# Linear stage of a two-layer transformer: the output projection in three bf16 passes on a split gated activation

## The reference

```python
q = jax.nn.softmax(q, axis=-1)
k = jax.nn.softmax(k, axis=1)
ctx = jnp.einsum('bnhd,bnhl->bhdl', k, v)
y = jnp.einsum('bnhd,bhdl->bnhl', q, ctx).reshape(B, T, D)
emb_out = jax.nn.silu(emb) @ emb_W + emb_b
scale, shift = jnp.split(emb_out, 2, axis=-1)
h = layer_norm(y, sn_g, sn_b) * (1.0 + scale) + shift
h = jax.nn.silu(h) @ out_W + out_b
return x + gate_msa * h
```

## Time and profile before

| | us |
|---|---|
| median of three runs | 1329.25 |
| lowest and highest of them | 1326.26, 1334.49 |
| the profiled execution | 1331.78 |
| its span, from first to last instruction | 1330.0 |
| PE busy in the span | 1172.4 (88%) |
| DVE busy | 945.9 (71%) |
| ACT busy | 784.2 (59%) |
| POOL busy | 846.9 (64%) |
| mean granted TensorE clock | 0.968 of full speed |

### The profile page before, as it was taken

How to read it: one execution, slowest core, us unless ns; L and a number is a source line. 1 busy time by engine, 2 the same in 40 slices (tenths; PEclk the granted TensorE clock), 3 DMA queues, 4 the chain that set the end, 5 groups by cost and what they waited for, 6 DMA issues and landing times. The chain is left out here.

```text
span 1330.0 us, 37647 instructions
## 1 busy us (share of the span) xinstructions
PE 1172.4 (88%) x12222; PEld 857.5 (64%) x12222; DVE 945.9 (71%) x2275; ACT 784.2 (59%) x2143; POOL 846.9 (64%) x1026
## 2 busy tenths in 40 slices
PE   3578898989989884699999999996899999999996
PEld 2356777777777773366666666673566666666664
DVE  3857787878878753764645565624899999999984
ACT  1466676777777762345545454632576767777664
POOL 2556677777777754636666666641467676767677
PEclk9789999999999997699999999997999999999999
DMA  5554233232322322100110101010011111111112
GB/s 160 146 125 105 50 58 62 53 60 56 58 61 54 64 54 71 52 17 16 33 32 16 32 16 32 17 33 0 12 32 43 39 51 39 35 55 35 39 55 73
DMA packets 142576, 67.86 MB, mean 51 GB/s; under 512 B 80432, under 2 KB 141232, under 8 KB 142512
## 3 DMA queue, kind: packets, MB, share of 16 engines
q1 hardware_dynamic: 109904, 40.92, 13.8%
q10 hardware_dynamic: 32608, 26.12, 6.9%
HBM read 41.31 MB, written 8.65 MB: 38 GB/s over the span
## 5 line engine op out<-in xcount | busy, mean ns | idle before, releaser
L1140 PE MATMUL f_ps_h<-f_x_split,w_fc 128*128 128x512 bf16 x768 | 172.9, 382 | 2.2 <-DVE f_biases L1267 1.2
L1113 PE MATMUL f_ps_y<-w_fc,f_h_split 128*128 128x256 bf16 x1536 | 172.7, 273 | 2.3 <-DVE f_branch L1232 2.3
L1113 PEld LDWEIGHTS f_ps_y<-w_fc,f_h_split 128*128 128x128 bf16 x1536 | 150.1, 98 | 23.6 <-issue 3.0
L625 POOL TENSOR_TENSOR e_split<-e_full,e_split 128x1024 bf16<-128x1024 f32 x64 | 136.6, 2134 | 34.1 <-ACT e_full L698 32.8
L1240 DVE TENSOR_TENSOR f_h_split<-f_h,f_h_split 128x512 bf16<-128x512 f32 x64 | 62.5, 979 | 105.9 <-ACT f_h L1097 105.9
L1140 PEld LDWEIGHTS f_ps_h<-f_x_split,w_fc 128*128 128x128 bf16 x768 | 75.4, 98 | 88.8 <-issue 2.8
L1096 ACT ACTIVATE f_h_split<-f_ps_h,b_fc 128x512 bf16<-128x512 f32 x128 | 89.1, 696 | 66.3 <-POOL f_h_split L1047 37.0
L758 PE MATMUL ps_s<-qk_t,k_pairs 128*128 128x64 bf16 x3072 | 102.3, 194 | 13.1 <-DMA k_pairs<-qk_t 10.5
L607 POOL TENSOR_TENSOR x_split<-x_t,x_split 128x256 bf16<-128x256 f32 x64 | 44.5, 696 | 104.3 <-ACT x_split L647 104.3
L758 PEld LDWEIGHTS ps_s<-qk_t,k_pairs 128*128 128x128 bf16 x3072 | 99.7, 99 | 15.9 <-DMA k_pairs<-qk_t 12.0
L1445 POOL TENSOR_TENSOR l_rstd<-l_mean_var,eps_norm 128x2 f32<-128x2 f32 (+1 forms) x73 | 14.1, 194 | 139.0 <-DVE l_mean_var L1638 107.5
(11 more groups left out here) (184 smaller groups left out, 3293.0 us busy)
## 6 DMA issues: line engine op xcount, KB each, us to landing
v_pairs<-v_split SPq DMA_DIRECT2D x128, 66.0 KB, 2.1
k_pairs<-qk_t SPq DMA_DIRECT2D x256, 32.0 KB, 2.2
gain<-gammas SPq DMA_DIRECT2D x64, 128.0 KB, 3.0
f_gain<-gammas ACTq DMA_DIRECT2D x32, 256.0 KB, 4.3
l_gate<-in_cond ACTq DMA_DIRECT2D x128, 64.0 KB, 2.6
out<-x_all ACTq DMA_DIRECT2D x16, 512.0 KB, 3.0
x_all<-in_x SPq DMA_DIRECT2D x13, 512.0 KB, 6.2
w_ada<-in_L_cond_ada_w SPq DMA_DIRECT2D x1, 1536.0 KB, 8.4
```

The costliest lines, as they stand in the source:

```text
L625: pool.tensor_tensor(flat(e_split[a][:, LO]), flat(e_full[:]), flat(e_split[a][:, HI]), ALU.subtract).then_inc(e_lo_made, 1)
L1113: last = pe.matmul(ps_y[:, i], h_split[a][:, hs, f, i * P:(i + 1) * P], m.w_fc2[:, ws, f], start=(f == 0 and k == 0), stop=(f == F_CHUNKS ...
L1140: last = pe.matmul(ps_h[f % 4][:], m.w_fc1[:, ws, c, f * P:(f + 1) * P], x2_split[a][:, xs, c], start=(k == 0 and c == 0), stop=(k == 2 an ...
```

## The change

Three edits go together.

1. `w_out3` becomes a pair of bf16 halves. The f32 weights are loaded into an unused part of `fc1_full`, and in the feed-forward pass, in front of the split of the q, v and k weights of the linear pass, ACT writes the high half and DVE the low half.
2. In the linear pass the sum of the gated activation stays on POOL in f32. A new stage `silu_high` (lag 10) on ACT copies it to bf16, and a new stage `silu_low` (lag 10) on POOL subtracts this copy from the f32 value and writes the rest in bf16.
3. `project` multiplies by `SPLITS`: six bf16 matmuls in place of two f32 ones, behind the same bias matmul. It waits for `silu_lo_made`.

```diff
-        self.w_out3 = sb("w_out3", [P, NC_, C], F32)
+        self.w_out3 = sb("w_out3", [P, 2, NC_, C], BF16)
...
-            sp.dma_start(m.w_out3[:], out_w.rearrange(CHUNKED, p=P)).then_inc(m.linear_here, 16)
+            sp.dma_start(out3_full, out_w.rearrange(CHUNKED, p=P)).then_inc(out3_here, 16)
...
                 if isinstance(t.n, int) and t.n == 2:
+                    act.wait_ge(out3_here, 16)
+                    act.activation(m.w_out3[:, HI], out3_full, ACT.Copy).then_inc(out3_hi_made, 1)
...
                 if isinstance(t.n, int) and t.n == 2:
+                    dve.wait_ge(out3_hi_made, 1)
+                    dve.tensor_tensor(m.w_out3[:, LO], out3_full, m.w_out3[:, HI], ALU.subtract)
...
                 pool.wait_ge(tanh_made, t.n + 1)
-                reuse(pool, out_done, t, 2)
                 pool.tensor_tensor(silu[a][:], tanh[a][:], z_t[a][:], ALU.mult).then_inc(silu_product, 1)
...
+            def silu_low(t):
+                a = t.slot(2)
+                pool.wait_ge(silu_hi_made, t.n + 1)
+                reuse(pool, out_done, t, 2)
+                pool.tensor_tensor(silu_split[a][:, LO], silu[a][:], silu_split[a][:, HI], ALU.subtract
+                                   ).then_inc(silu_lo_made, 1)
...
-                            (10, silus), (12, add)])
+                            (10, silus), (10, silu_low), (12, add)])
...
+            def silu_high(t):
+                a = t.slot(2)
+                act.wait_ge(silu_made, t.n + 1)
+                reuse(act, out_done, t, 2)
+                act.activation(silu_split[a][:, HI], silu[a][:], ACT.Copy).then_inc(silu_hi_made, 1)
...
-                           (3, k_exponentials), (9, modulate), (3, q_exponentials), (13, store),
+                           (3, k_exponentials), (9, modulate), (3, q_exponentials), (10, silu_high), (13, store),
...
-                pe.wait_ge(silu_made, t.n + 1)
+                pe.wait_ge(silu_lo_made, t.n + 1)
...
-                for c in range(NC_):
-                    last = pe.matmul(ps_out[:], silu[a][:, c], m.w_out3[:, c], start=False, stop=(c == NC_ - 1))
+                for i, (zs, ws) in enumerate(SPLITS):
+                    for c in range(NC_):
+                        last = pe.matmul(ps_out[:], silu_split[a][:, zs, c], m.w_out3[:, ws, c],
+                                         start=False, stop=(i == 2 and c == NC_ - 1))
```

More of the change, by code:

```diff
@@ L932, in feed_forward_pass @@
         b_norm3_wide = m.fc1_full[:, :, 0:P]
+        out3_full = m.fc1_full[:, :, D_FF - C:D_FF]
         minus_g_norm3 = sb("minus_g_norm3", [P, NC_], F32, 1)[0]
@@ L950, in feed_forward_pass @@
         qvk3_here = sem("qvk3_here")
+        out3_here = sem("out3_here")
+        out3_hi_made = sem("out3_hi_made")
         qvk3_hi_made = sem("qvk3_hi_made")
@@ L1001, in _ @@
                 sp.dma_start(biases3[:, k * C:(k + 1) * C], source[None, :].to_broadcast([P, C])).then_inc(qvk3_here, 16)
-            sp.wait_ge(m.linear_here, 16 * 3)
+            sp.wait_ge(m.linear_here, 16 * 2)
         @block.gpsimd
@@ L1245, in widen_norm3 @@
                 if isinstance(t.n, int) and t.n == 0:
-                    dve.wait_ge(m.linear_here, 16 * 3)
+                    dve.wait_ge(m.linear_here, 16 * 2)
                     dve.tensor_copy(b_norm3_wide, m.b_norm3[:, :, None].to_broadcast([P, NC_, P])
@@ L1324, in linear_pass @@
         silu = sb("silu", [P, NC_, P])
+        silu_split = sb("silu_split", [P, 2, NC_, P], BF16)
         gate = sb("gate", [P, C], F32, 4)
@@ L1372, in linear_pass @@
         silu_made = sem("silu_made")
+        silu_hi_made = sem("silu_hi_made")
+        silu_lo_made = sem("silu_lo_made")
         out_done = sem("out_done")
```

## The result

The changed kernel takes 1390.61 us (median; 1389.08 to 1397.95) beside 1331.87 us of the kernel before, measured again on the same chip. The ratio is 1.0459, 95% interval 1.0411 to 1.0508. The prediction was 1385 us in a range of 1366 to 1402, slower by more than 1% with a chance of 0.96. It was right.

A forecast was written before the change was run, and what follows sets the result against it. PE bound the kernel at 6.05 us per step; a new 6.92 us ring would replace it. Links 49.6 plus ends 1.3 and 5.2 on 1331.8 gave 1387.9, less 2.5 for the median 1385.4 us; range 1366 to 1402.

The forecast's parts named there:

- The new ring: Linear pass, one-step loop softmax, transposes, ACT's body, `silu_high`, `silu_low`, addition, next softmax: 6.92 us sets the step; chance 0.80.
- PE's saving: Projection on PE: six bf16 matmuls take 0.66 us where f32 took 0.87, so 0.21 less per tile.
- ACT's 3.16: Part of the new ring: ACT from the copy of k to the tanh's slot, which `silu_high` takes, 3.16 us.
- the handover: Part of the new ring: `silu_high` on ACT 0.41 us, then 0.08 until POOL starts `silu_low`.
- the 57 links: Linear pass, step 11 to step 68: 342.7 us before, 392.3 with the new ring, +49.6.
- the last link: Last of the 57 links: its ACT part has no exponentials, so 1.47 us less than 6.92.
- The end of the pipeline: Steps 68 to 73, paced by POOL's chain: 7.6 us more, less 2.2 absorbed by waits and 0.2 from projection, +5.2.
- Weights at nothing: Feed-forward pass: moved weight transfer and the two splits, 0.75 us each, taken as 0; +1.5 once without cover.
- The nearest other ring: Before the change, two-step loop through DVE's mean of y, POOL, PE and DVE's turn of 5.64: 11.42 us, 5.71 per step.
- PE's rival: Linear pass: PE stays the bound and 0.21 is saved in 57 links; about 1324 us, or 1317 with ends hidden; chance 0.04.
- The two-step ring alone: Rival: only the two-step ring binds, grown by 1.26 to 12.68 us, 6.34 per step; 1353 us; chance 0.08.
- PE as the bound: Same claim as PE's rival: PE stays the bound, not slower, about 1324 us; chance 0.04.

The follow-up runs named there:

- experiment 4: Changed kernel with ScalarE's copy `silu_high` one place earlier, ahead of the exponential of q: 1377.07 us, ratio 1.035 to the kernel before.
- experiment 11: Changed kernel with only GpSimd's addition to x moved behind the softmax products: 1352.85 us, ratio 1.0158 to the kernel before.
- experiment 1: Changed kernel with `silu_high` first in ScalarE's step and `silu_low` right behind GpSimd's softmax products (both lag 11): 1326.15 us, ratio 0.9964 to the kernel before.
- experiment 6: Changed kernel without ScalarE's copy; GpSimd writes the sum in bf16 and in f32, then subtracts: 1380.27 us, ratio 1.0377 to the kernel before.
- experiment 7: Experiment 1 with VectorE's sums of q's exponentials ahead of the normalised x: 1322.82 us, ratio 0.9942 to the kernel before.
- experiment 9: Experiment 1 with GpSimd's addition to x moved behind the next step's softmax products (lag 13): 1329.13 us, ratio 0.9977 to the kernel before.
- experiment 10: Experiment 1 with GpSimd's addition behind the softmax products and VectorE's sums ahead of the normalised x: 1319.50 us, ratio 0.9913 to the kernel before.
- experiment 3: Changed kernel without copy and subtraction; GpSimd's sum writes bf16, and PE's six passes use the high half for the low: 1322.64 us, ratio 0.9947.
- experiment 12: Kernel before, f32 projection kept, with GpSimd's addition behind the softmax products and VectorE's sums ahead of the normalised x: 1328.36 us, ratio 0.997.
- experiment 5: Changed kernel with ScalarE's copy `silu_high` ahead of the modulation and the exponential of q: 1418.22 us, ratio 1.0655 to the kernel before.
- experiment 2: Changed kernel with only GpSimd's subtraction moved behind the next step's softmax products (lag 11): 1336.17 us, ratio 1.0044 to the kernel before.

## Why the prediction was right

*The new ring* was named with its members and its length, 6.92 us; the profile shows the same members and 7.02. Three runs change only the places of instructions, two by taking one instruction out of the ring, one by cutting it. Taking out 0.31 gave a step of 6.74 (experiment 4), taking out the addition's 0.69 gave 6.32 (experiment 11), and the cut with the copy early gave 5.98 (experiment 1). Engine load explains none of it, since the instructions were the same in all.

*The terms.* PE's saving, 0.21: measured 0.22. ACT's 3.16 from the copy of k to the slot of `silu_high`: 3.16. `silu_low`: 0.63 to the next start, predicted 0.65. The one term too small is the handover. `silu_high` and its gap were priced at 0.49 from the earlier trace rows; in the step above it is 1158.17 - 1157.55 = 0.62, in others 0.55, on the mean of the 57 links 0.59. That makes +0.10 per step, 5.6 of the 8.5 us by which the 57 links were underrated. Of the rest some 2.5 us are steps in which PE's clock was lower (last section), and the last link took 5.92, not 6.92 - 1.47 = 5.45. The end of the pipeline costs 7.3, predicted 5.2; I had let GpSimd's waits absorb 2.2 of 7.6, and they absorbed nearly nothing. Still inside the bounds given.

*Weights at nothing* was wrong. I looked at the transfer and at the two splits, and not at who had waited for the transfer. DVE's wait for it at the start of the feed-forward pass is gone, and that is 5.0 us less. So part of the hit is luck: this gain, which I didn't have, makes up for nearly half of the 8.5 and 2.1 us that links and end were too small. Without it the median would be near 1396 (an estimate, 1390.6 + 5.0), still in the range. DVE's split took 1.23 us where I took 0.75.

*The nearest other ring*, 5.71 us per step before, was wrong. I took VectorE's turn at its busy time. In experiment 6 it contains the wait for the halves of x behind PE's products. That experiment's 13.3 us, less the 1.52 that it adds on GpSimd, gives 11.8 for two steps, and experiment 7 shows 11.83. VectorE's own turn with its wait for the inverse deviation was missing too: experiments 1, 7, 9 and 10 together put it at 5.98, though no row adds its length up. So the value for PE's rival (all of 0.21 saved) was also wrong: with the orders of before the runs give only 0.08 of it (experiments 1 and 3). It had no part in the forecast, since 6.92 was far above either. PE's own queue before is 6.02 (experiment 12), not 6.05, and the new one 5.81, not 5.84.

*Another ring of one step* was missed, through the tanh and the high half of x. I asked only whether the copy needs the sum in time, not who stands behind the copy if it doesn't come. In the changed kernel it is 6.03 by estimate, and hidden; experiment 5 ran into it, and experiment 2 as far as its rows tell.

*The rivals.* The two-step ring alone at 6.34 falls: the steps are 7.03 on the mean, PE waits for softmax in 44 of 48 of them, and ScalarE's wait for the sum is not among the long waits. PE as the bound falls by the same rows.

The Trainium skill, "Perfetto Trace Analysis", section "Optimizing Scalar/DVE Operations", says that offloading some work to ScalarE or GpSimd may make sense when VectorE is saturated. These runs put a condition to it: with the same two instructions on ScalarE and GpSimd the kernel is 4.6% slower than before at one place of the queues and 0.4% faster at another, and the 0.4% is no more than what the weights' wait gives.

## What to carry to other kernels

Idle time of an engine is room only for work that may stand in that idle time. Before adding an instruction with a wait, write down what stands behind it on its queue and follow that until you come back to the instruction; if you come back after one step, the sum of that way is a floor under the step, whatever the busy shares say. Take the parts of such a ring from start to start with their waits in, not from busy times; hand over between engines one step later, where both sides idle, and when one ring is removed look for the next before counting the gain. When a transfer or a semaphore changes place, list every wait that counted on it, in the earlier stages too.

## What the runs showed that was not expected

A handover from ScalarE to GpSimd isn't one number. The copy alone takes 0.42 us and the subtraction starts 0.50 after the copy's start (961.81 and 962.31 us in the changed kernel). In a full queue the same copy records 0.47 and the subtraction starts 0.62 or 0.55 later. Which part of the 0.1 is the queue and which the loop's code ahead of the subtraction isn't settled; no run separates them.

In the changed kernel PE is no longer busy all the time, and its granted clock is no longer full all the time: 0.98 as a mean from 957 to 1360 us, before 1.00. It falls in short stretches, to 0.83 on the mean of this one:

```profile
1280.00:1300.00 20.00, 17.72 (x135) 11.71 (x136) 15.00 (x44) 12.53 (x54) 12.80 (x22) 0.83 0.14 46
```

The steps there last 7.77, 7.29 and 7.29 us, and two others, from 1103.10 and 1188.18 us on, 7.66 and 7.67; ahead of and in these two the clock is 0.80 and 0.86 from 1095 to 1105 us and 0.83 and 0.82 from 1180 to 1190. Against their neighbours the five are some 2.5 us in all. In the step from 1103.10 ScalarE's copy comes 3.47 us after the copy of k, not 3.16: there it does wait for the sum, for GpSimd had to wait 2.15 us for the mean of y. So a slower PE costs little here, in five steps of 57. Why the clock falls there is not shown.
